# First attention of a gated cross-attention stack: TensorE begins a turn with the first scores, then the context half of the projection, then the first key scores

## The reference

```python
x = x + jnp.tanh(g_xattn[0]) * _L0_xattn_ref(_layernorm(x), ctx_2048, Wq, Wk, Wv, Wsk, Wsv, Wo)

def _L0_xattn_ref(hidden_states, ssm_states, ...):
    q = _heads(jnp.concatenate([ssm_states, hidden_states], axis=-1) @ Wq, H)      # 32 heads of 8
    k, v = _heads(hidden_states @ Wk, HK), _heads(hidden_states @ Wv, HK)          # 8 heads of 8
    ssm_k, ssm_v = _heads(ssm_states @ Wsk, HK), _heads(ssm_states @ Wsv, HK)
    # keys and values of both are joined; scores + alibi bias, masked to windows of 64 and 32,
    # softmax, times the values
    return o.transpose(0, 2, 1, 3).reshape(B, T, HID) @ Wo
```

## Time and profile before

| what | value |
|---|---|
| median of 3 timed runs | 1287.36 us (1286.54 to 1288.73) |
| profiled execution, its own time | 1293.26 us |
| its span in the trace | 1291.4 us |
| TensorE busy (matmuls) | 1067.4 us, 83% |
| VectorE busy | 840.1 us, 65% |
| ScalarE, GpSimd busy | 536.7 us, 535.8 us |

### The profile page before, as it was taken

The page is one execution under the profiler, slowest core; times in us unless marked ns, Lnnn a source line. Parts: engine busy times, 40 slices in busy tenths (PEclk is TensorE's granted clock), DMA queues, the critical chain, the costliest instruction groups (busy, mean ns, idle before and its releaser), DMA issues.

```text
span 1291.4 us, 32522 instructions
## 1 busy us (share of the span) xinstructions
PE 1067.4 (83%) x11717; PEld 825.5 (64%) x11717; DVE 840.1 (65%) x2315; ACT 536.7 (42%) x1058; POOL 535.8 (41%) x1053
## 2 busy tenths in 40 slices
PE   4898898995587388886989789999946779978898
PEld 2576676774476144443666567777735569968798
DVE  2665675765554588985666657787756757755475
ACT  2454455554354267665000024333311544346432
POOL 2444554654884888731000113223143425610261
PEclk9899898997799599998999989999968989989999
DMA  5321323410575654541000010000020610134331
GB/s 188 126 94 63 130 92 132 165 40 34 159 213 164 152 143 141 145 121 73 1 1 0 12 30 18 24 24 16 9 66 9 200 54 34 74 115 149 110 108 62
DMA packets 105788, 112.67 MB, mean 87 GB/s; under 512 B 12548, under 2 KB 95636, under 8 KB 104892
## 3 DMA queue, kind: packets, MB, share of 16 engines
q1 hardware_dynamic: 96732, 88.47, 21.9%
q0 software_dynamic: 8064, 22.06, 5.7%
q10 hardware_dynamic: 864, 0.43, 0.1%
HBM read 66.07 MB, written 44.84 MB: 86 GB/s over the span
## 4 chain that ended last, share of the span: by engine, by line
PE 57%; DVE 14%; issue 9%; ACT 7%; DMA 6%; POOL 5%; SPq 2%; DVEq 0%; ACTq 0%; POOLq 0%
PE psum L2686 5%; DMA PT<-xs 4%; PE psum L1087 3%; DVE mx L857 2%; ACT PT L2340 2%; PE psum L2397 2%; PE psum L1019 2%; ACT ext L2349 2%; PE psum L1686 2%; PE psum L1021 2%; PE psum L1070 2%; POOL rstd L762 2%; PE psum L1688 2%; PE psum L1687 2%; PE psum L1050 2%
## 5 line engine op out<-in xcount | busy, mean ns | idle before, releaser
L760 POOL TENSOR_SCALAR veps<-mv 128x1 f32<-128x1 f32 x112 | 33.5, 299 | 292.0 <-DVE mv L747 155.4
L857 DVE TENSOR_REDUCE mx<-psum 128x6 f32<-128x960 f32 (+3 forms) x80 | 80.7, 1009 | 66.9 <-PE psum L1055 65.8
L738 POOL DMA_INDIRECT got<-ys,rows_y x64 | 63.6, 994 | 118.6 <-DMA ys<-yt 94.6
L944 ACT ACTIVATE PT<-psum 128x1024 f32<-128x1024 f32 x64 | 65.5, 1024 | 70.5 <-PE psum L1075 70.5
L2300 DVE TENSOR_REDUCE mx<-psum 128x4 f32<-128x1024 f32 x64 | 77.0, 1206 | 19.8 <-PE psum L2371 19.0
L2340 ACT ACTIVATE PT<-psum 128x1024 f32<-128x1024 f32 x64 | 65.5, 1023 | 34.3 <-PE psum L2382 33.6
L1686 PE MATMUL psum<-xnTh,w7h 128*128 128x256 f32 x256 | 75.5, 295 | 1.3 <-issue 0.7
L2111 DVE SCALAR_TENSOR_TENSOR x<-psum,cw,x 128x256 f32 (+1 forms) x128 | 53.0, 476 | 36.2 <-PE psum L2059 36.0
L1688 PE MATMUL psum<-xnTh,w7l 128*128 128x256 f32 x256 | 73.6, 288 | 0.0
L1687 PE MATMUL psum<-xnTl,w7h 128*128 128x256 f32 x256 | 73.5, 287 | 0.0
L2686 PE MATMUL psum<-mskp,ident_r 128*128 128x512 f32 x256 | 70.6, 411 | 2.9 <-ACT PT L2637 1.6
(11 more groups left out here) (418 smaller groups left out, 3415.2 us busy)
## 6 DMA issues: line engine op xcount, KB each, us to landing
xs<-qpad SPq DMA_DIRECT2D x17, 1024.0 KB, 5.1
PT<-xs SPq DMA_DIRECT2D x78, 128.0 KB, 2.1
ys<-yt SPq DMA_DIRECT2D x78, 128.0 KB, 2.1
ctxT<-in_ctxT SPq DMA_DIRECT2D x48, 128.0 KB, 2.3
ext<-qscr SPq DMA_DIRECT2D x96, 64.0 KB, 2.5
arena<-in_w SPq DMA_DIRECT2D x4, 1280.0 KB, 9.9
w_raw<-in_w SPq DMA_DIRECT2D x12, 384.0 KB, 3.6
q_parts<-kscr SPq DMA_DIRECT2D x66, 64.0 KB, 2.2
```

Source lines behind the costliest of these rows:

```text
L738: pool.indirect_dma_start(out=dst[:, t % 4, k], out_offset=None, in_=ys[:], in_offset=bass.IndirectOffsetOnAxis(ap=rows_y[:, t, k:k + 1], ...
L857: V.tensor_reduce(mx0[:, u0:u0 + m].rearrange("p j e -> p e j"), src, axis=AX.X, op=ALU.max, negate=True).then_inc(F("mx").sem, 1)
L944: A.activation(PT[:, 1024 * r:1024 * (r + 1)], bank(6, 2), ACT.Exp).then_inc(F("p").sem, 1)
```

## The change

`project` is cut in two. The x half stays at the end of a turn. The context half goes to the next turn, where the same item is called n, behind the first scores. The first key scores go behind it. The wait for `mxT` stays first; no matmul, copy or wait is added or taken away.

```diff
-            def project(m, s, turn):
-                wait(f"ctx_loaded{s}", turn, 16)
+            def project_x(m, s):
                 wait("xnT", m, 1)
                 for c in range(NC):
                     MM(bank(0)[:, 128:512], xnT[:, s, c, 0:T], w0x[:, c], start=(c == 0), stop=False, skip_group_check=True)
+
+            def project_context(m, s, turn):
+                wait(f"ctx_loaded{s}", turn, 16)
                 for c in range(NC):
                     t = MM(bank(0)[:, 0:384], ctxT[:, s, c], w0c[:, c], start=False, stop=(c == NC - 1), skip_group_check=True)
                 t.then_inc(F("qkv_psum").sem, 1)
...
                 if among(p):
                     wait("mxT", p, 1)
-                    key_scores(p, 1 - s, 0)
                 if among(b):
...
                     wait("qkT", b, 3)
                     scores(b, s, 0)
+                if among(n):
+                    project_context(n, 1 - s, n // 2)
+                if among(p):
+                    key_scores(p, 1 - s, 0)
                 ft = i - 3
                 if among(n):
                     wait("qkv", n, 2)
...
                 if among(m):
-                    project(m, s, half_i + 1)
+                    project_x(m, s)
```

## The result

The changed kernel takes **1293.89 us** (median of 15 runs), the kernel before 1287.77 beside it (15 runs): a ratio of 1.005, with a 95% interval of 1.0034 to 1.0065. It is slower, by 6.1 us. The forecast was 1293.4, 6.0 slower.

The account below looks back on a forecast made before the run. TensorE's own queue was taken to set the pace. Thirteen full turns add 5.3 us and the remaining terms bring it to 6.0, so 1287.4 + 6.0 = 1293.4 us, range 1288.2 to 1297.0.

Parts of the forecast that it names:

- Step 1: Scores 0, moved ahead of the context half, start without a wait; their inputs are ready with 0.57 and 0.2 us left.
- Step 2: The context half ends 0.50 us later: 0.34 for scores 0 plus 0.16 for two added changes of matmul kind.
- Step 3: A new TensorE wait of 0.34 us opens before `pvT`, as scores 0 no longer cover the copy for `qkv`.
- Step 4: Earlier maxima 0 remove the wait before scores 1; scores 2 come 0.15 us earlier from `pvT`, 0.07 with places.
- The sum for a clean turn: A turn without a stop lengthens by 0.50 - 0.15 us, or 0.50 - 0.07 with places.
- The stops: Stops of about 4 us in turns 4, 7 and 10 stay, ending with the weight load, 0.50 us later each.
- The remaining turns: Other full turns lengthen by 0.50 less 0.15 or 0.07; turn 0 by 0.15, turn 1 0.50, turn 15 0.3 us.
- the chain of clears: Near the end, a stop of about 1 us is bound to clears, taking about 0.3 us off the sum.
- Rival A: Instruction fetch gets ahead of the weight load, gaining 5.5 us per stop; two stops gone gives 1282.4 us, chance 0.04.
- Rivals B and C: B: both waits go, 1281 us, chance 0.03. C: free kind changes, most of 0.34 regained, 1288.7 us, chance 0.11.
- Rival D: TensorE's clock falls to 1.2 GHz behind the new waits each turn, costing 20 us, 1313 us, chance 0.04.

Follow-up runs that it names:

- The transposes in between: Kernel before, with the four full-array bf16 maxima transposes moved between x half and context half: 1291.49 us in a single execution.
- Scores-first: Kernel before, with scores 0 moved ahead of key scores 0 only and the projection left whole: 1268.32 us, ratio 0.9875.
- late weights: Kernel before, with SyncE issuing the weights of turns 1, 4, 7 and 10 only behind scores 4: 1296.96 us, ratio 0.9899 beside 1313.15.

## Why the prediction was right, point by point

**Step 1, scores 0 can start at once: right.** They follow the x half with no wait, 1.45 behind its start.

**Step 2, 0.50 later: right, 0.53.** x half to scores 0 takes 1.45, where x half to context half took 1.34: +0.11. Scores 0 take 0.32, the context half 1.49 instead of 1.39: +0.10. The terms were put at 0.34 + 0.16; they measure 0.32 + 0.21, so part of the match is that the two errors cancel. The transposes in between showed that the 0.10 at the end of the x half comes with the 64-row tiles; the start of the context half behind such tiles costs 0.10 too, where the prediction had 0.06 from a start behind full-array matmuls. All these distances repeat to 0.01 us in the thirteen full turns.

**Step 3, the new wait of 0.34: right.** `kv_f` starts 131.17 - 130.78 = 0.39 behind the start of key scores 0, and `pvT` starts 0.81 behind them, where their own 0.46 would have ended. That is 0.35. The trace names `kv_f` as the releaser and puts 0.18 to it, since it counts from the end of the row before (131.02 + 0.39), and such a row reaches past the start of the next one where nothing waits (130.78 + 0.40 against 131.02); the distance of starts is the measure here. The kernel with the wait behind scores 1 gets back 0.25 of it, the only direct test.

**Step 4, the gain of 0.15 and 0.07: right.** From `pvT` to scores 2 is 2.79 (131.59 to 134.38) instead of 2.95, and in turns with places 0.09 less. Scores-first, which has this gain and no other edit, shows 0.16 and 0.08 in turn lengths.

**The sum for a clean turn: right.** 0.50 - 0.15 = 0.35 was forecast and 0.37 measured; 0.43 and 0.45 with places.

**The stops: right that they stay, wrong in their price.** I had put 0.50 on each of turns 4, 7 and 10. They cost +1.2, -0.1 and -0.2, together 1.0 instead of 1.5. The step that failed is that a stop "is 0.50 later whatever was gained before it". By the split above, the end of the stop comes 0.60, 0.0 and 0.7 later: 1.3 together, near the forecast but not by turn. What stands behind it changes by +0.65, -0.1 and -0.9. That is the slow stretch, which the sum left out and whose length isn't fixed: at the lower clock TensorE works for 3.4 and 5.1 us behind the stop of turn 4 before and 6.0 and 5.5 after, and in turn 10 for 5.0 and 5.6 before and 3.4 and 3.4 after. The part behind the stop is about half of that longer or shorter. Why the stretch is long in one turn and short in another was not tried.

**The remaining turns: wrong in size.** Turns 3, 6, 9, 12 and 13 gave +0.31, +0.28, +0.18, +0.24 and -0.24, 0.8 us together, where the sum had 1.9 less 0.3 for the chain of clears. Turn 1 gave +0.64 for +0.5, turn 15 +0.20 for +0.3. The maxima transposes of turn 0 start 0.53 and 0.37 us earlier in the changed kernel, where +0.15 was forecast; what does this was not tried. The short stop of turn 13, which the prediction bound to a chain of clears, stands at instruction 7617, again 1792 on, so it is a stop of the same kind; it shrank from 1.11 and 0.57 us to 0.18 and about as much, which is why this turn got shorter. So the first attention comes to about 4.2 us in the traces instead of 6.0. That the timed difference is 6.1 is within its interval, and in part luck.

**Rival A**, that a fetch gets ahead of the weights, didn't happen in this change, but its mechanism is real, and its size of 5.5 us a stop is right (17.5 for three, with the small gain of the order in it). I had weighed it by lateness: 4 us late against 0.50 us of delay. That reasoning was wrong. Moving scores 0 by one place in a neighbouring order brought the fetch 8 us forward. A chance of 0.04 came out all right here; for the order next to it, it would have been a bad miss. The reading of the earlier trace rows, that the stop ends with the landing of the weights, holds only as a coincidence in time. In turns 7 and 10 TensorE goes on at 154.72 and 208.74, 0.4 us before the weights have landed (issued at 144.62 and 199.05, landing 10.5 and 10.1 later), and with late weights a stop ends before they are issued. In turn 4 the packet starts at 98.35, 2.2 us before the landing, and TensorE goes on 2.37 us behind its start (2.30 in the changed kernel, 2.77 with late weights). What the late weights do show is that the transfers of the head hold it back.

**Rivals B and C** needed `qkv` hidden or the changes of kind free: neither is so. **Rival D**: the clock is at 1.00 in the clean turn, with a new wait of 0.35 and one of 0.55 in it.

## What to carry to other kernels

Before work is moved ahead of a projection, ask what it covers where it stands: here 0.34 us of scores hid the end of a 0.80 us copy, and moving them cost that 0.34 at once, and 0.2 for two more changes of tile, and brought 0.15, since the next consumer stood behind another operation of the same engine. Leaving both small pieces behind the whole projection and only swapping them gave the same gain for no price. And where an engine stands for microseconds with no releaser, look at the instruction queue and at what large transfers were issued ahead of it: three such stops were worth over 1%, more than twice what the order of the work was. What brings the fetch forward isn't known here, so a reordering has to be measured and not reckoned.

## What the runs showed of the hardware beyond this

- **TensorE's code comes by DMA and can be late.** A packet of the instruction queue q8 that starts at 98.35 us, behind 2.3 MB of clears and weights that were issued 7 to 8 us before, goes with a stop of TensorE of 4 us and a granted clock of 0.50 (1.2 GHz) for 3 to 6 us after it: about 6 us a stop. It goes with an early fetch (16 to 17 us less for three, by ratio and by medians), and shrinks to 1.08 us with 1.25 MB less ahead of it. The Trainium skill, Runtime: NRT & Kernel Launch, section Instruction fetch mechanics, says that the next block of 256 instructions is fetched on a queue of the sequencer's own while the current one runs, and that this is mostly hidden. The trace agrees with the block: in every kernel with the stops 2241, 4033 and 5825 recorded instructions of TensorE stand before them, each 193 above a multiple of 256, also where added instructions moved them in the program. It doesn't agree that the cost is hidden: with large transfers on the same DMA engines it isn't.
- **When the next block is asked for stays open.** One or four instructions more, and a semaphore instruction at the place of scores-first's, did not take the stops away; taking that one out of scores-first did nothing either. The order of key scores 0, scores 0 and the two halves decides, and I don't know by what.
- **A change to 64-row tiles costs 0.10 us** behind fp32 matmuls of the full array, and a start of these behind full-array bf16 ones about 0.06, behind 64-row ones 0.10, at full clock.
